# One cross-attention layer on one core: the last batch's output projection is spread over its second pass

## The chip, the core and the metric

The kernel runs on one core of a Trainium2 chip. A core has five engines that run their own instruction streams in order and meet only through semaphores: TensorE (PE) multiplies, with its weight loads shown apart as PEld; VectorE (DVE) and ScalarE (ACT) work on the results; GpSimd (POOL) does copies and subtractions; SyncE (SP) issues most of the DMAs. TensorE writes to PSUM, which has eight banks; the kernel uses all of them. The metric is the device time of one execution in microseconds (us), the median of the runs.

## The reference, cut to what matters

```python
# x, ctx: (8, 256, 1024) float32; Wq, Wout: (1024, 1024); 32 heads of 32
xn = (x - mu) * rsqrt(var + eps) * gamma + beta
Q = split_heads(xn @ Wq.T); K = V = split_heads(ctx)
scores = einsum('bhsd,bhtd->bhst', Q, K) * scale
probs  = softmax(where(mask, scores, -inf))
attn   = einsum('bhst,bhtd->bhsd', probs, V)
return x + attn.reshape(B, S, HIDDEN) @ Wout.T
```

## The kernel before, in words

The eight batches (B = 8) go through a software pipeline, one `iteration` each. The 32 heads are taken four at a time, in G = 8 groups g; a group fills one 128-row slice k = g of the attention result. To keep float32 accuracy with float16 matmuls, `aT`, `woT`, `qT` and the others are kept as a high and a low part, and a product takes three matmuls (`PASSES`).

An iteration has two passes. **First pass**, STEPS = 16 steps n: `scores_s` puts four 128x256 score matmuls into one of the two `score` tiles (score0, score1 in turn, two PSUM banks each); DVE takes the maxima (L826, `max_step`), ACT the exponentials with their sums (L653, `row_sums`). From those come the logarithms of the sums: `lse_half` and `lse_rows` on DVE, `l_transposes` on PE, and `fill_l_rows` on SP, six small DMAs (L203) into `q_stack`, three for each half of the groups. **Second pass**, for each g: `scores_t` twice (L525, four matmuls each, waiting until ACT has emptied the score tile), ACT's `exp_step` twice (L670), then `probs_times_v` (L537) into pv0 or pv1, ACT's copy to `aT` (L676, high part) and DVE's subtraction (L861, low part, semaphore `a_lo`). PE issues `probs_times_v` of g-1 behind the scores of g. ACT issues the copy of g-2 behind the two exponentials of g.

**The output projection** of a batch is 4 tiles of 128x512 (i = 0 to 3), each the sum of 8 slices by 3 passes = 24 matmuls of 512 columns (O_MM = 24, O_ALL = 96). `o_matmuls` (L478) issues them by a unit count u in the order of O_ORDER into the banks mm0 and mm1, i even and odd. `add_residual` (L868) on DVE adds x, `load_res` and `store_out` on SP bring x and take the result. Tiles 2 and 3 wait until the sums of tiles 0 and 1 have been read out of their banks (`o_done`). In the middle of the program the output of batch b-1 is spread over the first pass of batch b, and the query projection of batch b+1 over the second.

In the last iteration (b = 7) there is no next batch. There the output of batch 6 is issued 5 matmuls a step (O_AT_LAST), 80 in all, and the other 16 behind the last step, ahead of the second pass. DVE adds its tiles behind steps 8, 10 and 15 and the fourth behind the loop (O_ADDS_LAST). SP has the store of tile 2 of batch 6 queued ahead of the six L203 DMAs, which the second pass waits for (semaphore l_in). The last batch's own output is 15 matmuls between the `probs_times_v` of groups 6 and 7, and 81 behind that of group 7.

Every wait is written out by hand, and each engine's order is the order of the code.

Of the kernel before, what the change touches and what calls it, by code (L numbers as in the profile page):

```python
# [15 lines left out]
B, S, D = 8, 256, 1024  # L16
H = 32
DH = D // H
P = 128
KT = D // P  # L20
ST = S // P
J = P // DH
G = H // J
LN_EPS = 1e-5
SCALE = float(DH) ** -0.5
W_SCALE = 8.0
# [6 lines left out]
PASSES = ((0, 0), (0, 1), (1, 0))  # L33
FILLS = 4
STEPS = G * ST
# [10 lines left out]
def xattn(nc, x, ctx_in, mask, wq, wout, gamma, beta, out):  # L46
    es = ExitStack()
    with es:
        def sb(name, shape, dt):
            return es.enter_context(nc.sbuf_tensor(name, shape, dt))  # L50

        def sem(name):
            return es.enter_context(nc.semaphore(name))

        wqT = sb("wqT", [P, 2, KT, D], F16)
        woT = sb("woT", [P, 2, KT, D], F16)
# [5 lines left out]
        aT = sb("aT", [P, 2, G, S], F16)  # L62
# [3 lines left out]
        res = sb("res", [P, 2, 512], F32)  # L66
        o_buf = sb("o_buf", [P, 2, 512], F32)
# [27 lines left out]
        score = [es.enter_context(nc.psum_tensor(f"score{i}", [P, J, S], F32)) for i in range(2)]  # L95
        pv = [es.enter_context(nc.psum_tensor(f"pv{i}", [P, 2, S], F32)) for i in range(2)]
        mm = [es.enter_context(nc.psum_tensor(f"mm{i}", [P, 512], F32)) for i in range(2)]
# [22 lines left out]
        t_ready, exp_done, pv_ready = sem("t_ready"), sem("exp_done"), sem("pv_ready")  # L120
        a_hi, a_lo = sem("a_hi"), sem("a_lo")
        o_ready, o_done = sem("o_ready"), sem("o_done")
# [22 lines left out]

        def known(b, n):
            return isinstance(b, int) and b == n

        @block.sync
        def _(sp):  # L150
# [203 lines left out]
        def _(pe):  # L354
# [103 lines left out]
            O_MM = KT * 3  # L458
            O_ORDER = [(0, k) for k in range(7)] + [(1, k) for k in range(4)] + [(0, 7)] + [(1, k) for k in range(4, 8)]
            O_ORDER += [(i, k) for i in (2, 3) for k in range(KT)]  # L460

            def o_matmuls(c, lo, hi, q_before):
                for u in range(lo, hi):
                    (i, k), p = O_ORDER[u // 3], u % 3
                    v = 3 * k + p
                    st, nh = i // 2, i % 2
                    if u == 0:
                        pe.wait_ge(a_lo, c * G + 5)
                    if u in (3 * O_ORDER.index((0, 5)), 3 * O_ORDER.index((0, 6)), 3 * O_ORDER.index((0, 7))):
                        pe.wait_ge(a_lo, c * G + k + 1)  # L470
                    if v == 0 and i >= 2:
                        pe.wait_ge(o_done, c * FILLS + i - 1)
                    elif v == 0 and q_before:
                        pe.wait_ge(q_lo, (c + 1) * FILLS + i + 3)
                    elif v == 0:
                        pe.wait_ge(o_done, (c - 1) * FILLS + i + 3)
                    ap, wp = PASSES[p]
                    last = pe.matmul(mm[i % 2][:], aT[:, ap, k, st * P:(st + 1) * P], woT[:, wp, k, nh * 512:(nh + 1) * 512],  # L478
                                     start=(v == 0), stop=(v == O_MM - 1))
                    if v == O_MM - 1:  # L480
                        last.then_inc(o_ready, 1)

            def scores_s(b, pb, n, first):
                g, st = n // 2, n % 2
                h, gl = divmod(g, HALF)
                if n in (0, STEPS // 2):
                    pe.wait_ge(k_in[h], (b + 1) * (STACK + 1) * DMA)
                if known(b, 0) and n == 0:
                    pe.wait_ge(q0_in, STACK * DMA)
                elif n == (4 if known(b, 0) and h == 0 else h * STEPS // 2):  # L490
                    pe.wait_ge(q_in[h], (b + 1) * STACK * DMA)
                if n >= 2:
                    pe.wait_ge(sum_done, b * STEPS + n - 1)
                elif not first:
                    pe.wait_ge(exp_done, b * STEPS + n - 1)
                else:
                    pe.wait_ge(wq_lo, W_FILLS - 2 + 2 * n)
                for j in range(J):
                    last = pe.matmul(score[n % 2][:, j, :], q_stack[0:S_ROWS, h, j, gl, st * P:(st + 1) * P], k_stack[0:S_ROWS, pb, h, j, gl, :],  # L499
                                     start=True, stop=True)  # L500
                last.then_inc(s_ready, 1)
# [27 lines left out]
            def probs_times_v(b, pb, g):  # L529
                pe.wait_ge(exp_done, b * STEPS + 2 * g + 2)  # L530
                if g < 2:
                    pe.wait_ge(l_done, (b * 2 + g + 1) * L_STEPS)
                else:
                    pe.wait_ge(a_lo, b * G + g - 1)
                for tt in range(ST):
                    for j in range(J):
                        last = pe.matmul(pv[g % 2][DH * j:DH * (j + 1), 0, :], ctx_sb[:, pb, tt, g * P + DH * j:g * P + DH * (j + 1)],  # L537
                                         probs[:, g % 2, tt, j, :], start=(tt == 0), stop=(tt == ST - 1), skip_group_check=True)
                last.then_inc(pv_ready, 1)

            O_ALL, Q_ALL = 4 * O_MM, 4 * Q_MM
            O_AT = [min(7 * n, O_ALL) for n in range(STEPS + 1)]
            Q_AT_STEP = [0] * 14 + [0, 14, 28]
            Q_AT = [60 + 16 * g for g in range(G)] + [182, Q_ALL]
            O_AT_LAST = [5 * n for n in range(STEPS + 1)] + [O_ALL] * (G + 2)
            Q_AT_STEP_FIRST = [0] * 6 + [9 * n for n in range(11)]
            Q_AT_FIRST = [104 + 11 * g for g in range(G)] + [187, Q_ALL]

            def iteration(b, pb, first, last):
                c = None if first else b - 1  # L550
                for n in range(STEPS):
                    scores_s(b, pb, n, first)
                    if not last:
                        if n in Z_STEPS:
                            z_transposes(b + 1, Z_STEPS.index(n), b)
                        if n in K_STEPS:
                            k_transposes(b + 1, 1 - pb, K_STEPS.index(n), b)
                    if first and n in WO_STEPS:
                        wo_transposes(WO_FIRST + WO_STEPS.index(n))
                    if not first:  # L560
                        at = O_AT_LAST if last else O_AT
                        o_matmuls(b - 1, at[n], at[n + 1], True)
                    if not last:
                        at = Q_AT_STEP_FIRST if first else Q_AT_STEP
                        q_matmuls(b + 1, at[n], at[n + 1], c)
                    if n == L_STEP:
                        l_transposes(b, 0, last)
                q_at = Q_AT_FIRST if first else Q_AT
                q_done = Q_AT_STEP_FIRST[STEPS] if first else Q_AT_STEP[STEPS]
                if last:  # L570
                    o_matmuls(b - 1, O_AT_LAST[STEPS], O_AT_LAST[STEPS + 1], True)
                else:
                    q_matmuls(b + 1, q_done, q_at[0], c)
                for g in range(G):
                    scores_t(b, pb, 2 * g)
                    scores_t(b, pb, 2 * g + 1)
                    if not last:
                        q_matmuls(b + 1, q_at[g], q_at[g + 1], c)
                    if g == 0:
                        l_transposes(b, 1, last)  # L580
                    if g >= 1:
                        probs_times_v(b, pb, g - 1)
                if not last:
                    q_matmuls(b + 1, q_at[G], q_at[G + 1], c)
                else:
                    o_matmuls(b, 0, 5 * 3, False)
                probs_times_v(b, pb, G - 1)

            pe.wait_ge(ident_ok, 1)
# [29 lines left out]
            for b in range(1, B - 1, 2):  # L619
                iteration(b, 1, False, False)  # L620
                iteration(b + 1, 0, False, False)
            iteration(B - 1, 1, False, True)
            o_matmuls(B - 1, 5 * 3, O_ALL, False)

        @block.scalar
        def _(act):
# [116 lines left out]
        def _(dve):  # L743
# [119 lines left out]
            def add_residual(c, i):  # L863
                dve.wait_ge(o_ready, c * FILLS + i + 1)
                dve.wait_ge(res_in[i % 2], (c * 2 + i // 2 + 1) * DMA)
                if i >= 2:
                    dve.wait_ge(out_done[i % 2], (c * 2 + 1) * DMA)
                dve.scalar_tensor_tensor(out=o_buf[:, i % 2, :], in0=mm[i % 2][:], scalar=1.0 / W_SCALE, in1=res[:, i % 2, :],  # L868
                                         op0=ALU.mult, op1=ALU.add).then_inc(o_done, 1)

            def iteration(b, first, last, more):
# [45 lines left out]
                    q_split(b + 1, 3)  # L917
                att_split(b, G - 1)

            O_ADDS, O_ADDS_LAST = (6, 8, 11, 14), (8, 10, 15)  # L920
            for r, unit in enumerate(L_UNITS + (1.0,)):
                dve.memset(rows[0:1, r, :], unit).then_inc(consts, 1)
            row_stats(0, 0)
# [7 lines left out]
            for i in range(FILLS):  # L931
# [3 lines left out]
                for m in range(2):  # L935
                    k = 2 * i + m
                    last = dve.tensor_scalar(z0_f32[:, i, m, :], bank[:, m, :], gb[:, 0, k:k + 1], gb[:, 1, k:k + 1], ALU.mult, ALU.add)
# [50 lines left out]
```

## Time and profile before

| | us |
|---|---|
| median of 3 runs | 629.6 (628.39 to 630.53) |
| the profiled execution, its own time | 630.62 |
| its span, first to last instruction | 628.8 |
| last iteration, from the first scores (549.94) to the end | 78.9 |
| of it behind the last attention product's start (606.90) | 21.9 |

Times in the rows below are counted from the start of the span. The trace shows one execution, whose own time is 1.0 us above the median; between span and own time lie 1.8 us. Matmul durations in it are modelled with their drain, so that a group's length is more than its share of the engine; the distance between starts is what the engine takes.

### The profile page before, as it was taken

Reading aid. Unit: us, or ns where it says so; the run is one execution under the profiler, and the core shown is the slowest. Engines: PE = TensorE matmul, PEld = TensorE weight load, DVE = VectorE, ACT = ScalarE, POOL = GpSimd, SP = SyncE. Lnnn points to the kernel's source line nnn. Section 1 sums busy time; section 2 is a strip of 40 time slices with the busy share of each in tenths; the row PEclk is TensorE's granted clock in tenths of the full one; section 3 lists DMA queues with packets and bytes.
Section 4 is the critical chain, followed back from the end, with each engine's and each line's share of the span. In section 5 each row is a group of like instructions: output and inputs, shape, how many; then the busy total and the mean of one; then the engine's idle time right before and its main releaser. Section 6 shows DMA issues by size and latency. Waiting matters only on the chain.

```text
span 628.8 us, 12852 instructions
## 1 busy us (share of the span) xinstructions
PE 589.5 (94%) x4769; PEld 396.2 (63%) x4769; DVE 385.0 (61%) x841; ACT 430.8 (69%) x1321; POOL 112.8 (18%) x131
## 2 busy tenths in 40 slices
PE   4878879999999999999999999999999999998897
PEld 4667657655776567655776567755776567644443
DVE  5575977478654885388654886288645882278211
ACT  3342978778766886678766886678666885699740
POOL 2320440035000530044000520044001520000000
PEclk9889689999999999999999999999999999999899
DMA  9774321443344252343344152333344132321202
GB/s 282 267 223 128 114 73 55 122 126 99 106 117 130 60 163 56 107 117 105 100 125 130 52 170 57 99 119 109 96 124 134 63 89 57 98 51 67 71 1 101
DMA packets 37344, 68.62 MB, mean 109 GB/s; under 512 B 9009, under 2 KB 11041, under 8 KB 37282
## 3 DMA queue, kind: packets, MB, share of 16 engines
q1 hardware_dynamic: 36994, 67.60, 35.9%
q8 instruction: 38, 0.62, 0.4%
q10 hardware_dynamic: 288, 0.20, 0.1%
q14 instruction: 24, 0.20, 0.1%
HBM read 33.56 MB, written 8.39 MB: 67 GB/s over the span
## 4 chain that ended last, share of the span: by engine, by line
PE 71%; DVE 14%; ACT 8%; issue 3%; DMA 2%; ACTq 1%; SPq 1%; DVEq 0%
PE mm L453 24%; PE mm L478 17%; PE pv L537 10%; PE score L525 9%; PE score L499 6%; DVE nmax L826 6%; ACT score L653 6%; PE pv L415 2%; PE pv L428 2%; DMA ctx_sb<-in_ctx 1%; ACT probs L670 1%; DVE o_buf L868 1%; PE pv L382 1%; DVE wqT L748 1%; DVE t_f L777 1%
## 5 line engine op out<-in xcount | busy, mean ns | idle before, releaser
L653 ACT ACTIVATE score<-score,nmax 128x256 f32<-128x256 f32 x512 | 230.1, 465 | 47.7 <-DVE nmax L826 47.6
L453 PE MATMUL mm<-zT,wqT 128*128 128x256 f16 x1536 | 186.6, 276 | 0.0
L826 DVE TENSOR_REDUCE nmax<-score 128x2 f32<-128x512 f32 x256 | 163.8, 684 | 37.0 <-PE score L499 36.9
L478 PE MATMUL mm<-woT,aT 128*128 128x512 f16 x768 | 183.6, 379 | 1.5 <-DVE o_buf L868 1.5
L670 ACT ACTIVATE probs<-score 128x1024 f32<-128x1024 f32 x128 | 123.9, 1022 | 73.4 <-PE score L525 73.1
L453 PEld LDWEIGHTS mm<-zT,wqT 128*128 128x128 f16 x1536 | 151.5, 99 | 23.0 <-issue 2.9
L478 PEld LDWEIGHTS mm<-woT,aT 128*128 128x128 f16 x768 | 74.7, 97 | 73.2 <-DVE o_buf L868 4.4
L653 ACT ACTIVATION_READ_ACCUMULATOR score<-score,nmax 128x1 f32 x512 | 114.7, 224 | 0.0
L861 DVE TENSOR_TENSOR aT<-pv,aT 128x256 f16<-128x256 f32 x64 | 26.9, 423 | 114.7 <-ACT aT L676 113.9
L499 PE MATMUL score<-k_stack,q_stack 97*128 97x256 f16 x512 | 79.6, 279 | 10.5 <-ACT score L653 9.4
L499 PEld LDWEIGHTS score<-k_stack,q_stack 97*128 97x128 f16 x512 | 47.9, 99 | 46.4 <-ACT score L653 22.9
L326 POOL CAST zT<-t_f 128x512 f16<-128x512 f32 x28 | 17.1, 609 | 322.0 <-DVE t_f L769 322.0
L525 PE MATMUL score<-q_stack,k_stack 100*128 100x256 f16 x512 | 68.3, 276 | 2.0 <-ACT probs L670 1.1
L537 PE MATMUL pv<-probs,ctx_sb 128*32 128x256 f32 x1024 | 69.4, 389 | 0.9 <-DVE aT L861 0.6
L525 PEld LDWEIGHTS score<-q_stack,k_stack 100*128 100x128 f16 x512 | 45.7, 98 | 29.2 <-issue 18.1
L537 PEld LDWEIGHTS pv<-probs,ctx_sb 128*32 128x32 f32 x1024 | 27.5, 110 | 25.9 <-ACT probs L670 8.0
L645 ACT ACTIVATE qT<-mm 128x512 f16<-128x512 f32 x32 | 19.5, 608 | 23.0 <-PE mm L453 23.0
L782 DVE SCALAR_TENSOR_TENSOR qT<-mm,qT 128x512 f16<-128x512 f32 x32 | 22.0, 689 | 20.5 <-ACT qT L645 20.0
L328 POOL TENSOR_TENSOR zT<-t_f,zT 128x512 f16<-128x512 f32 x28 | 32.3, 1155 | 2.2
L338 POOL TENSOR_TENSOR kT<-t_f,kT 128x512 f16<-128x512 f32 x28 | 32.3, 1155 | 2.2
L868 DVE SCALAR_TENSOR_TENSOR o_buf<-mm,res 128x512 f32<-128x512 f32 x32 | 21.7, 679 | 17.3 <-PE mm L478 17.3
L676 ACT ACTIVATE aT<-pv 128x256 f16<-128x256 f32 x64 | 24.8, 390 | 9.0 <-PE pv L537 9.0
(62 smaller groups left out, 352.2 us busy)
## 6 DMA issues: line engine op xcount, KB each, us to landing
k_stack<-kT SPq DMA_DIRECT2D x192, 64.0 KB, 2.0
q_stack<-qT SPq DMA_DIRECT2D x180, 64.0 KB, 2.0
x_nat<-in_x SPq DMA_DIRECT2D x8, 1024.0 KB, 5.4
ctx_sb<-in_ctx SPq DMA_DIRECT2D x8, 1024.0 KB, 6.3
res<-in_x SPq DMA_DIRECT2D x32, 256.0 KB, 2.9
out<-o_buf SPq DMA_DIRECT2D x32, 256.0 KB, 2.0
probs<-in_L_xattn_Wq SPq DMA_DIRECT2D x8, 512.0 KB, 7.8
probs<-in_L_xattn_Wout SPq DMA_DIRECT2D x8, 512.0 KB, 4.5
```

Of the source, the lines that this page charges most:

```text
L328: pool.tensor_tensor(zT[:, 1, at], t_f32[:, f % 2], zT[:, 0, at], ALU.subtract).then_inc(split_done, 1)
L338: pool.tensor_tensor(kT[:, 1, at], t_f32[:, f % 2], kT[:, 0, at], ALU.subtract).then_inc(split_done, 1)
L453: last = pe.matmul(mm[i % 2][:, m2 * S:(m2 + 1) * S], wqT[:, wp, k, m * P:(m + 1) * P], zT[:, zp, k, :], start=(v2 == 0), stop=(v2 == KT * ...
L478: last = pe.matmul(mm[i % 2][:], aT[:, ap, k, st * P:(st + 1) * P], woT[:, wp, k, nh * 512:(nh + 1) * 512], start=(v == 0), stop=(v == O_M ...
L499: last = pe.matmul(score[n % 2][:, j, :], q_stack[0:S_ROWS, h, j, gl, st * P:(st + 1) * P], k_stack[0:S_ROWS, pb, h, j, gl, :], start=True ...
L525: last = pe.matmul(score[n % 2][:, j, :], k_stack[0:T_ROWS, pb, h, j, gl, tt * P:(tt + 1) * P], q_stack[0:T_ROWS, h, j, gl, :], start=True ...
L537: last = pe.matmul(pv[g % 2][DH * j:DH * (j + 1), 0, :], ctx_sb[:, pb, tt, g * P + DH * j:g * P + DH * (j + 1)], probs[:, g % 2, tt, j, :] ...
L653: last = act.activation(score[n % 2][:, j, :], score[n % 2][:, j, :], ACT.Exp, bias=nmax[:, st, h, j, gl:gl + 1], accum_out=sums[:, st, h, ...
L670: act.activation(probs[:, g % 2, tt], score[n % 2][:], ACT.Exp).then_inc(exp_done, 1)
L826: dve.tensor_reduce(nmax[:, st, h, at, gl], score[n % 2][:, at, :], AX.X, ALU.max, negate=True).then_inc(max_done, 1)
L861: dve.tensor_tensor(aT[:, 1, g, :], pv[g % 2][:, 0, :], aT[:, 0, g, :], ALU.subtract).then_inc(a_lo, 1)
L868: dve.scalar_tensor_tensor(out=o_buf[:, i % 2, :], in0=mm[i % 2][:], scalar=1.0 / W_SCALE, in1=res[:, i % 2, :], op0=ALU.mult, op1=ALU.add ...
```

## The change

`o_last` and the order `O_GROW` are new; `o_bank` gives tiles 2 and 3 of the last batch the two halves of score0, on PE and on DVE. The output of batch 6 is issued 6 matmuls a step, all 96 in the first pass. DVE adds its tiles behind steps 5, 9 and 13, the fourth behind the loop as before. In the second pass, from g = 2, a piece of six matmuls of the last batch's own output follows `probs_times_v` of g-1: three for tile 0 and three for tile 1, both of slice k = g-2, behind a wait for that slice's `a_lo`. Slices 6 and 7, and the 48 matmuls of tiles 2 and 3, follow the last attention product.

```diff
+        def o_bank(c, i):
+            if known(c, B - 1) and i >= 2:
+                return score[0][:, 2 * i - 4:2 * i - 2].rearrange("p j s -> p (j s)")
+            return mm[i % 2][:]
...
+            O_GROW = [(i, k) for k in range(KT) for i in (0, 1)] + [(i, k) for i in (2, 3) for k in range(KT)]
+            def o_last(lo, hi):
+                c = B - 1
+                for u in range(lo, hi):
+                    (i, k), p = O_GROW[u // 3], u % 3
+                    v = 3 * k + p
+                    st, nh = i // 2, i % 2
+                    if i == 0 and p == 0:
+                        pe.wait_ge(a_lo, c * G + k + 1)
+                    if v == 0 and i < 2:
+                        pe.wait_ge(o_done, (c - 1) * FILLS + i + 3)
+                    elif u == 2 * O_MM:
+                        pe.wait_ge(exp_done, B * STEPS - 1)
+                    ap, wp = PASSES[p]
+                    last = pe.matmul(o_bank(c, i), aT[:, ap, k, st * P:(st + 1) * P], woT[:, wp, k, nh * 512:(nh + 1) * 512],
+                                     start=(v == 0), stop=(v == O_MM - 1))
+                    if v == O_MM - 1:
+                        last.then_inc(o_ready, 1)
...
-            O_AT_LAST = [5 * n for n in range(STEPS + 1)] + [O_ALL] * (G + 2)
+            O_AT_LAST = [6 * n for n in range(STEPS + 1)]
...
-                if last:
-                    o_matmuls(b - 1, O_AT_LAST[STEPS], O_AT_LAST[STEPS + 1], True)
-                else:
+                if not last:
                     q_matmuls(b + 1, q_done, q_at[0], c)
...
+                    if last and g >= 2:
+                        o_last(6 * (g - 2), 6 * (g - 1))
...
-                else:
-                    o_matmuls(b, 0, 5 * 3, False)
                 probs_times_v(b, pb, G - 1)
...
-            o_matmuls(B - 1, 5 * 3, O_ALL, False)
+            o_last(6 * (G - 2), O_ALL)
...
-                dve.scalar_tensor_tensor(out=o_buf[:, i % 2, :], in0=mm[i % 2][:], scalar=1.0 / W_SCALE, in1=res[:, i % 2, :],
+                dve.scalar_tensor_tensor(out=o_buf[:, i % 2, :], in0=o_bank(c, i), scalar=1.0 / W_SCALE, in1=res[:, i % 2, :],
...
-            O_ADDS, O_ADDS_LAST = (6, 8, 11, 14), (8, 10, 15)
+            O_ADDS, O_ADDS_LAST = (6, 8, 11, 14), (5, 9, 13)
```

PE in the second pass of the last batch, before: the scores of one group (into score0 and score1), the attention product of the group ahead of it, and the scores of the next group.

```order
L525 MATMUL score0<-q_stack,k_stack 128x256 [waits exp_done]
L525 MATMUL score0<-q_stack,k_stack 128x256 x3
L525 MATMUL score1<-q_stack,k_stack 128x256 [waits exp_done]
L525 MATMUL score1<-q_stack,k_stack 128x256 x3
L537 MATMUL pv1<-probs,ctx_sb 32x256 [waits a_lo,exp_done]
L537 MATMUL pv1<-probs,ctx_sb 32x256 x7
L525 MATMUL score0<-q_stack,k_stack 128x256 [waits exp_done]
L525 MATMUL score0<-q_stack,k_stack 128x256 x3
```

The same place in the changed kernel, whose line numbers are 28 higher at the scores and the attention product, and where L485 is the matmul of `o_last`.

```order
L553 MATMUL score0<-q_stack,k_stack 128x256 [waits exp_done]
L553 MATMUL score0<-q_stack,k_stack 128x256 x3
L553 MATMUL score1<-q_stack,k_stack 128x256 [waits exp_done]
L553 MATMUL score1<-q_stack,k_stack 128x256 x3
L565 MATMUL pv1<-probs,ctx_sb 32x256 [waits a_lo,exp_done]
L565 MATMUL pv1<-probs,ctx_sb 32x256 x7
L485 MATMUL mm0<-woT,aT 128x512 [waits a_lo]
L485 MATMUL mm0<-woT,aT 128x512 x2
L485 MATMUL mm1<-woT,aT 128x512 x3
L553 MATMUL score0<-q_stack,k_stack 128x256 [waits exp_done]
L553 MATMUL score0<-q_stack,k_stack 128x256 x3
```

Six output matmuls and a wait for `a_lo` now stand ahead of the next group's scores.

DVE at the end of the last batch's first pass, before: the maxima of steps 13, 14 and 15, then the sums of tiles 2 and 3 of batch 6, then `lse_half`.

```order
L826 TENSOR_REDUCE nmax<-score 128x2 [waits s_ready]
L826 TENSOR_REDUCE nmax<-score 128x2
L826 TENSOR_REDUCE nmax<-score 128x2 [waits s_ready]
L826 TENSOR_REDUCE nmax<-score 128x2
L826 TENSOR_REDUCE nmax<-score 128x2 [waits s_ready]
L826 TENSOR_REDUCE nmax<-score 128x2
L868 SCALAR_TENSOR_TENSOR o_buf<-mm,res 128x512 [waits out_done0,res_in0,o_ready]
L868 SCALAR_TENSOR_TENSOR o_buf<-mm,res 128x512 [waits out_done1,res_in1,o_ready]
```

The same place in the changed kernel.

```order
L852 TENSOR_REDUCE nmax<-score 128x2 [waits s_ready]
L852 TENSOR_REDUCE nmax<-score 128x2
L894 SCALAR_TENSOR_TENSOR o_buf<-mm,res 128x512 [waits out_done0,res_in0,o_ready]
L852 TENSOR_REDUCE nmax<-score 128x2 [waits s_ready]
L852 TENSOR_REDUCE nmax<-score 128x2
L852 TENSOR_REDUCE nmax<-score 128x2 [waits s_ready]
L852 TENSOR_REDUCE nmax<-score 128x2
L894 SCALAR_TENSOR_TENSOR o_buf<-mm,res 128x512 [waits out_done1,res_in1,o_ready]
```

The sum of tile 2 has moved ahead of the maxima of steps 14 and 15.

## Rows read from the trace of the kernel before

**Rows 1.** The page, part 1: busy us, share of the span, number of instructions
```profile
PE 589.5 (94%) x4769; PEld 396.2 (63%) x4769; DVE 385.0 (61%) x841; ACT 430.8 (69%) x1321; POOL 112.8 (18%) x131
```
**Rows 2.** Windows of the last batch: stretch, length, busy by engine, clock, DMA
```profile
551.50:582.50 31.00, 27.98 (x151) 13.35 (x150) 23.54 (x44) 30.05 (x132) 0.00 (x0) 1.00 0.22 68
```
**Rows 3.** Timeline, one first-pass step: start, length, engine, line, what [idle before]
```profile
557.18 0.61 PE L499 MATMUL score<-k_stack,q_stack 97*128 97x256 f16 x4
...
557.62 1.25 PE L478 MATMUL mm<-woT,aT 128*128 128x512 f16 x5
...
559.00 0.61 PE L499 MATMUL score<-k_stack,q_stack 97*128 97x256 f16 x4
```
**Rows 4.** Timeline, end of the first pass and start of the second
```profile
575.68 2.47 DVE L826 TENSOR_REDUCE nmax<-score 128x2 f32<-128x512 f32 x4
...
578.20 0.46 ACT L653 ACTIVATE score<-score,nmax 128x256 f32<-128x256 f32 x1
...
580.23 0.68 DVE L868 SCALAR_TENSOR_TENSOR o_buf<-mm,res 128x512 f32<-128x512 f32 x1
...
580.94 0.34 SPq L214 DMA_DIRECT2D out<-o_buf  x1
...
581.33 8.12 SPq L203 DMA_DIRECT2D q_stack<-l_rows  x6
...
582.26 0.23 ACT L663 ACTIVATE ln_e<-ln_s 128x32 f32<-128x32 f32 x1
...
584.41 1.05 PE L525 MATMUL score<-q_stack,k_stack 100*128 100x256 f16 x8 [0.89 <-DMA q_stack<-l_rows]
...
585.06 2.85 ACT L670 ACTIVATE probs<-score 128x1024 f32<-128x1024 f32 x3 [2.57 <-PE score L525]
```
**Rows 5.** Windows around the clock's fall, columns as in rows 2
```profile
583.50:587.00 3.50, 1.90 (x15) 1.19 (x14) 2.33 (x9) 1.94 (x3) 0.00 (x0) 1.00 0.04 9
587.00:590.40 3.40, 3.35 (x23) 1.42 (x24) 0.61 (x2) 1.94 (x2) 0.00 (x0) 0.51 0.04 7
590.80:603.50 12.70, 11.89 (x140) 6.28 (x138) 2.12 (x5) 12.42 (x17) 0.00 (x0) 1.00 0.16 57
```
**Rows 6.** The chain that ended last, behind the clock's fall: start, us, what
```profile
587.05 1.03 PE score L525 x4
588.09 1.86 PE pv L537 x16
589.95 0.83 PE score L525 x4
```
**Rows 7.** Timeline, the second pass at full clock
```profile
593.62 1.07 PE L537 MATMUL pv<-probs,ctx_sb 128*32 128x256 f32 x16 [0.21 <-DVE aT L861]
...
594.62 1.05 PE L525 MATMUL score<-q_stack,k_stack 100*128 100x256 f16 x8
...
595.27 1.94 ACT L670 ACTIVATE probs<-score 128x1024 f32<-128x1024 f32 x2
...
597.09 0.39 ACT L676 ACTIVATE aT<-pv 128x256 f16<-128x256 f32 x1
...
597.52 0.42 DVE L861 TENSOR_TENSOR aT<-pv,aT 128x256 f16<-128x256 f32 x1 [1.93 <-ACT aT L676]
...
598.09 1.07 PE L537 MATMUL pv<-probs,ctx_sb 128*32 128x256 f32 x16 [0.21 <-DVE aT L861]
```
**Rows 8.** Timeline, the tail
```profile
603.56 3.41 PE L478 MATMUL mm<-woT,aT 128*128 128x512 f16 x15
...
606.90 1.07 PE L537 MATMUL pv<-probs,ctx_sb 128*32 128x256 f32 x16
607.90 17.66 PE L478 MATMUL mm<-woT,aT 128*128 128x512 f16 x81
...
608.45 0.42 DVE L861 TENSOR_TENSOR aT<-pv,aT 128x256 f16<-128x256 f32 x1 [3.60 <-ACT aT L676]
...
625.60 0.69 DVE L868 SCALAR_TENSOR_TENSOR o_buf<-mm,res 128x512 f32<-128x512 f32 x1 [4.49 <-PE mm L478]
```

## The prediction, made before the changed kernel was run

> **What bounds the kernel now.** I read the page first: PE is busy for 94% of the span [rows 1], so what matters is where PE is not the limit, and that is the last batch, which has no next batch's projection to fill its waits. The windows show it: in the first pass of the last batch ACT is busy for 30.05 of 31.00 us and PE for 27.98 [rows 2]. Then the timeline of one step: scores start at 557.18, the five output matmuls at 557.62, the next scores at 559.00 [rows 3]. A step is 1.82 us long, set by ACT, and PE needs 0.44 for the scores and 5 x 0.216 = 1.08 for the five (81 of them in 17.66 us less one drain of 0.38 make 0.216 each [rows 8]). So PE rests 0.30 us a step.
>
> At the end of that pass a queue is the limit. DVE adds tile 2 of batch 6 at 580.23, SP stores it at 580.94, and only then issues the six L203 DMAs, from 581.33. The scores of the second pass wait for the first three of them until 584.41, and ACT, done with its logarithm work at 582.49 (582.26 + 0.23), stands idle for 2.57 us before its first exponential at 585.06 [rows 4].
>
> In the second pass a ring of latencies is the limit, not one engine's work. Attention product at 593.62, scores at 594.62, two exponentials from 595.27, the copy at 597.09, the subtraction at 597.52, next but one attention product at 598.09 [rows 7]: 4.47 us for two groups, 2.24 a group. The other group's scores and exponentials lie beside that ring. The tail is PE alone: 15 matmuls, the last attention product, 81 matmuls, up to 625.56 (607.90 + 17.66) [rows 8].
>
> **Term 1, the first pass.** Six matmuls a step make PE's work 0.44 + 1.30 = 1.74 us, still under ACT's 1.82 [rows 3]: cost nothing, with 0.08 us to spare. If the spacing is 0.223, as the 15 have it (603.56 to 606.90 [rows 8]), it is 1.78 and still fits. Upper bound: a twentieth of a us in each of 16 steps, 0.8 us. The 16 matmuls behind the last step are gone from there.
>
> **Term 2, the start of the second pass.** The sum of tile 2 moves ahead of the maxima of step 14. Those of steps 13 and 14 begin at 575.68 and take 2.47 us for four [rows 4], so the sum starts at 575.68 + 1.24 = 576.92. It led to the L203 DMAs 1.10 us after its start and to the scores 4.18 us after it (580.23, 581.33, 584.41 [rows 4]). Moved, it gives scores at 581.10. Then that transfer is no longer last; ACT's own logarithm work is, at 582.49. What is queued behind the moved sum is the maximum of step 14: it starts at 576.92 + 0.68 = 577.60, its first half is done some 0.65 later, at 578.25, and ACT wanted it at 578.20 [rows 4]. I take 0.1 us for that, and 0.7 as the upper bound (all of the sum). The first exponential: 582.6 in place of 585.06, **a gain of 2.46 us**. The stores and loads of x queued on SP behind L203 only come earlier.
>
> **Term 3, the second pass.** Here the order of PE is what counts. The piece of slice g-2 stands behind the scores of g and ahead of the scores of g+1, and waits for `a_lo` of slice g-2. ACT makes that slice's copy only behind both exponentials of g. So the ring is now: scores of g, two exponentials, copy, subtraction, six matmuls, scores of g+1. Nothing of the next group can start beside it, since its scores are behind the wait. From rows 7: scores to exponentials 0.65 (594.62 to 595.27), exponentials to PE's release 2.82 (595.27 to 598.09), six matmuls 1.30. **One group takes 4.77 us in place of 2.24.** The attention product (1.00) lies in the 2.4 us in which PE waits for ACT and DVE, and costs nothing. ACT, busy for 12.42 of 12.70 us in this pass before [rows 5], now waits for PE some 2.5 us a group.
>
> The sum from the first `a_lo` on (593.62 before [rows 7]): five rings 5 x 4.77 = 23.85, the sixth piece 1.30, the last attention product 1.00, then 60 matmuls (slices 6 and 7 and the 48 in score0) 12.96; together 39.11. Slice 7 doesn't delay them: its `a_lo` is ready 2.12 us after the attention product's start (606.90 to 608.45, and 0.57 on to PE as from 597.52 to 598.09 [rows 7, 8]), and that product with slice 6's piece takes 2.30. Before, the same stretch was 593.62 to 625.56 = 31.94. **A loss of 7.17 us.** Below this could go only if PE got past the wait; above it, if a release takes longer (4.6 to 5.0 a ring as bounds, -0.9 to +1.1 in the sum).
>
> **Term 4, the clock.** PE's granted clock was 0.51 (1.2 GHz) from 587.0 to 590.4, after a stretch of 3.50 us in which PE was busy for 1.90; then it came back, PE having been busy without pause [rows 5]. It made three pieces of the path longer: 1.03 against 0.62 for scores, 1.86 against 1.00 for the attention product, 0.83 against 0.62, 1.5 us in all [rows 6]; the short ones are those of rows 3 and 8. In the changed kernel PE has its 16 leftover matmuls no longer, and from some 580.4 to 585.0 runs no more than the scores of two groups and two transposes, waiting for ACT in between. So I expect the same fall, 3 us earlier and at about the same price; it may hit a place where PE waits anyway. I take 0.3 us off. Bounds: -1.5 (it doesn't fall) to +0.5.
>
> **Tail.** The last sum and store are unchanged, and tile 2 comes 24 matmuls (5.2 us) ahead of tile 3 as before. Tiles 2 and 3 wait for nothing.
>
> **Sum:** -2.46 + 7.17 - 0.3 = +4.4 us. On the profiled execution's own 630.62 that is 635.0; on the median of 629.6 it is **634.0**. With every bound at its end, term 1's 0.8 and term 2's other 0.6 among them: from +2.3 to +7.7 us, 631.9 to 637.3.
>
> **Rival A: the clock falls within the rings too.** A ring keeps PE at work for 0.88 + 1.00 + 1.30 = 3.18 of 4.77 us, in two spells with a pause of 1.6 us; before, the second pass had it busy for 11.89 of 12.70 [rows 5] and the clock stayed up. The ring lies between that and the stretch of 583.5 to 587.0, after which it fell, and no row shows which it takes after. A fall doubles the six matmuls and the first scores of a ring, 1.7 us each time. One to four such rings: 1.7 to 7 us, with +4 as the middle: **638**. For it: the pauses come back in every ring. Against it: no single pause is as long as those of 583.5 to 587.0.
>
> The Trainium skill has a rule that speaks for this rival ("TensorE: Matmul & The Clock Gate", section "A second HAM failure mode: psum-queue depth-cycling"): pauses that return between groups of matmuls can make the clock go up and down, and the throughput is lost in the changes. The trace before has such short pauses in each first-pass step at full clock (0.30 of 1.82 us), so it doesn't bear the rule out for pauses of that size, and no row here has a pause of 1.6 us in every group. By that rule the time is the 638 of this rival.
>
> **Rival B, faster: the pieces hide in PE's waits.** That is what they would do if slice g-2 were ready when PE gets to its piece, that is 1.9 us after the scores of g started (0.88 and 1.00) and not 3.47. Then PE's own 3.18 us is the ring, 1.59 less, and five of them give 4.4 - 7.95 = -3.5 us: **626.1**. For it: ACT could copy slice g-2 ahead of g's exponentials, since its product is long done. Against it: the change leaves ACT's order as it is. It breaks even at a ring of 4.77 - 4.4/5 = 3.89 us.
>
> **Rival C: no difference.** The clock doesn't fall at all (-1.2 on my sum), and the rings take 4.5 us, because some release is quicker than in rows 7 (-1.35): +1.8, **631.4**. Each is possible, both together less so.
>
> **Rival D: the first pass no longer holds.** If six matmuls push the steps past ACT's 1.82 us, up to 0.8 us comes on top: 634.8. This lies in the forecast's own range, and has no chance of its own.
>
> **How the numbers follow.** Forecast (631.9 to 637.3) 0.61, rival A 0.23, rival C 0.10, rival B 0.06. A measurement of this kernel can tell about 0.3%, or 1.9 us, from no change. Faster is B, 0.06. Same is C, 0.10. Slower is the rest, 0.84. The range leaves out B and the dearer half of A: 631.0 to 638.5. The predicted time is that of the forecast, 634.0.
>
> **What the profile after would show.** Step by step: (1) first-pass steps still 1.82 us apart with six matmuls in each; a longer step is rival D. (2) L203 issued near 578, the first scores of the second pass near 581.1, ACT's first exponential at 582.6, released by nothing but ACT's own order; if it comes later, the delay of step 14's maximum was more than I took. (3) From then on scores of successive groups 4.8 us apart, PE idle before the pieces for 1.6 us with DVE's L887 subtraction as the releaser, and ACT's exponentials waiting for PE's scores; 3.2 us apart would be rival B. (4) The granted clock at 1.2 GHz once, near 584 to 588; more often and within the rings would be rival A. (5) The last matmul near 630 us of the span. I am wrong on the mechanism, not only on the size, if ACT doesn't wait for PE in the second pass.

## Result and profile after

The changed kernel takes **634.1 us** (median of 6 runs, 633.45 to 635.37), against 629.35 for the kernel before (6 runs, 628.12 to 630.53): a ratio of 1.0079, 95% interval 1.0062 to 1.0096. It is slower by 4.7 us. The forecast was 634.0.

The profiled execution has an own time of 633.76 us and a span of 632.0. In its lines L527 and L553 are the scores of the first and the second pass, L506 is an output matmul of batch 6, L696 an exponential of the second pass, L702 ACT's copy, L887 DVE's subtraction and L894 the sum with x.

The first pass and the start of the second, which [rows 3, 4] show of before. Timeline, columns as there (the first row is the last batch's first scores):

```profile
549.28 0.61 PE L527 MATMUL score<-k_stack,q_stack 97*128 97x256 f16 x4
...
552.88 0.61 PE L527 MATMUL score<-k_stack,q_stack 97*128 97x256 f16 x4
553.33 1.46 PE L506 MATMUL mm<-woT,aT 128*128 128x512 f16 x6
554.70 0.61 PE L527 MATMUL score<-k_stack,q_stack 97*128 97x256 f16 x4
...
576.27 0.67 DVE L894 SCALAR_TENSOR_TENSOR o_buf<-mm,res 128x512 f32<-128x512 f32 x1
...
577.35 9.26 SPq L210 DMA_DIRECT2D q_stack<-l_rows  x6
...
580.44 0.61 PE L553 MATMUL score<-q_stack,k_stack 100*128 100x256 f16 x4 [0.77 <-DMA q_stack<-l_rows]
...
581.79 1.92 ACT L696 ACTIVATE probs<-score 128x1024 f32<-128x1024 f32 x2
```

Steps are 1.82 us apart with six matmuls in each. Counted from the last batch's first scores, the second pass's first scores come 31.16 us in (before: 584.41 - 549.94 = 34.47) and the first exponential 32.51 us in (before: 585.06 - 549.94 = 35.12). ACT no longer stands idle ahead of that exponential.

One ring of the second pass, which [rows 7] show of before (timeline):

```profile
591.12 1.04 PE L553 MATMUL score<-q_stack,k_stack 100*128 100x256 f16 x8
591.76 1.94 ACT L696 ACTIVATE probs<-score 128x1024 f32<-128x1024 f32 x2 [2.46 <-PE score L553]
592.09 1.07 PE L565 MATMUL pv<-probs,ctx_sb 128*32 128x256 f32 x16
593.59 0.39 ACT L702 ACTIVATE aT<-pv 128x256 f16<-128x256 f32 x1
594.01 0.42 DVE L887 TENSOR_TENSOR aT<-pv,aT 128x256 f16<-128x256 f32 x1 [4.25 <-ACT aT L702]
594.49 1.47 PE L485 MATMUL mm<-woT,aT 128*128 128x512 f16 x6 [1.33 <-DVE aT L887]
595.80 1.04 PE L553 MATMUL score<-q_stack,k_stack 100*128 100x256 f16 x8
```

Scores, exponentials, copy, subtraction, six matmuls, scores: 4.68 us for this group (4.67 us between the starts of the pieces). Such a chain, in which each step waits for the one before and the last releases the first of the next group, is called a ring here. PE waits 1.33 us for DVE, ACT 2.46 us for PE. The waits of the second pass and the tail, added up (who waited for whom: us in all, times, longest):

```profile
ACT probs L696 <- PE score L553: 13.7, 7, 2.5
...
PE mm L485 <- DVE aT L887: 8.0, 6, 1.3
```

The tail, which [rows 8] show of before (timeline):

```profile
614.59 1.07 PE L565 MATMUL pv<-probs,ctx_sb 128*32 128x256 f32 x16
615.59 2.76 PE L485 MATMUL mm<-woT,aT 128*128 128x512 f16 x12
...
618.19 10.52 PE L485 MATMUL score<-woT,aT 128*128 128x512 f16 x48
...
628.75 0.69 DVE L894 SCALAR_TENSOR_TENSOR o_buf<-score,res 128x512 f32<-128x512 f32 x1 [4.49 <-PE score L485]
```

PE doesn't stall ahead of slice 7 or of the tiles in score0. The clock, in windows of 1 us (length, PE busy, clock, share and GB/s of DMA):

```profile
582.00:583.00 1.00, 0.56 (x4) 0.91 0.06 16
583.00:584.00 1.00, 1.00 (x6) 0.50 0.03 8
...
586.00:587.00 1.00, 1.00 (x14) 0.89 0.08 16
...
598.00:599.00 1.00, 0.00 (x0) 1.00 0.00 0
```

Before, it fell once too [rows 5]. Here it fell once, from 582.8 to 586.2, and stayed at 1.0 through the six pieces, each with a pause of PE ahead of it (the window from 598.00 lies wholly in one).

**A measure finer than the times.** Executions of one kernel differ by several us: the 21 of the kernel before that front_only is compared with run from 626.48 to 632.24. In the traces most of the difference comes from before the last batch: its first scores stand anywhere from 548.97 to 551.85. So all profiles are compared by the distance from those scores to the start of the last sum (L868 or L894).

| kernel | first scores | first exponential, from there | last sum, from there | clock fell in the last batch |
|---|---|---|---|---|
| before | 549.94 | 35.12 | 75.66 | once |
| changed | 549.28 | 32.51 | 79.47 | once |
| changed, again | 551.48 | 32.51 | 79.59 | once |
| front_only | 551.18 | 32.47 | 72.71 | once |
| growth_only | 550.65 | 35.12 | 80.97 | no |
| wait_only | 549.47 | 32.47 | 79.50 | once |
| early_copy | 550.08 | 32.47 | 69.92 | no |
| early_copy, again | 551.85 | 32.50 | 71.15 | once |
| lag_one | 551.40 | 32.48 | 71.81 | once |
| mm_banks | 549.76 | 32.48 | 79.84 | once |
| clock_kept | 549.13 | 32.47 | 78.30 | no |
| clock_kept, again | 549.30 | 32.50 | 78.32 | no |
| early_fill | 548.97 | 32.50 | 69.95 | no |
| early_fill, again | 550.37 | 32.50 | 69.95 | no |

By it the change costs 79.47 - 75.66 = 3.8 us. The line numbers of the variants below differ by a few from those of the changed kernel.

### The profile page after: what moved, and what is told of

The parts are those of the page before. It is cut to its first block, busy times and chain, and to the rows that moved or that the text cites. A ratio compares the mean times of both kernels' runs of the same rounds, so it can differ in the third digit from the quotient of the medians.

```text
span 632.0 us, 12852 instructions
## 1 busy us (share of the span) xinstructions
PE 587.6 (93%) x4769; PEld 396.8 (63%) x4769; DVE 385.6 (61%) x841; ACT 431.5 (68%) x1321; POOL 113.0 (18%) x131
## 4 chain that ended last, share of the span: by engine, by line
PE 73%; DVE 14%; ACT 7%; issue 3%; DMA 1%; ACTq 1%; SPq 0%; DVEq 0%
PE mm L460 23%; PE mm L506 16%; PE pv L565 9%; PE score L553 9%; PE score L527 7%; DVE nmax L852 6%; ACT score L679 4%; PE mm L485 2%; PE pv L422 2%; ACT probs L696 2%; PE score L485 2%; PE pv L435 2%; DMA ctx_sb<-in_ctx 1%; DVE o_buf L894 1%; DVE wqT L774 1%
## 5 line engine op out<-in xcount | busy, mean ns | idle before, releaser
L696 ACT ACTIVATE probs<-score 128x1024 f32<-128x1024 f32 x128 | 123.9, 1021 | 82.4 <-PE score L553 82.4
L506 PE MATMUL mm<-woT,aT 128*128 128x512 f16 x672 | 162.5, 379 | 1.5 <-DVE o_buf L894 1.5
L679 ACT ACTIVATION_READ_ACCUMULATOR score<-score,nmax 128x1 f32 x512 | 113.4, 221 | 0.0
L506 PEld LDWEIGHTS mm<-woT,aT 128*128 128x128 f16 x672 | 65.5, 97 | 61.4 <-DVE o_buf L894 4.4
L887 DVE TENSOR_TENSOR aT<-pv,aT 128x256 f16<-128x256 f32 x64 | 27.0, 424 | 125.1 <-ACT aT L702 124.4
L527 PE MATMUL score<-k_stack,q_stack 97*128 97x256 f16 x512 | 79.8, 279 | 8.4 <-ACT score L679 8.3
L527 PEld LDWEIGHTS score<-k_stack,q_stack 97*128 97x128 f16 x512 | 47.9, 99 | 43.2 <-ACT score L679 19.8
L553 PE MATMUL score<-q_stack,k_stack 100*128 100x256 f16 x512 | 68.1, 276 | 1.4 <-DMA q_stack<-l_rows 0.8
L553 PEld LDWEIGHTS score<-q_stack,k_stack 100*128 100x128 f16 x512 | 46.3, 98 | 27.3 <-issue 17.3
L702 ACT ACTIVATE aT<-pv 128x256 f16<-128x256 f32 x64 | 24.7, 389 | 8.1 <-PE pv L565 8.1
L795 DVE TENSOR_SCALAR t_f<-pv,gb 128x256 f32<-128x256 f32 x56 | 27.6, 535 | 0.0
```

Of the source, the lines that this page charges most:

```text
L553: last = pe.matmul(score[n % 2][:, j, :], k_stack[0:T_ROWS, pb, h, j, gl, tt * P:(tt + 1) * P], q_stack[0:T_ROWS, h, j, gl, :], start=True ...
L679: last = act.activation(score[n % 2][:, j, :], score[n % 2][:, j, :], ACT.Exp, bias=nmax[:, st, h, j, gl:gl + 1], accum_out=sums[:, st, h, ...
L696: act.activation(probs[:, g % 2, tt], score[n % 2][:], ACT.Exp).then_inc(exp_done, 1)
L795: last = dve.tensor_scalar(t_f32[:, f % 2, m, :], pv[f % 2][:, m, :], gb[:, 0, k:k + 1], gb[:, 1, k:k + 1], ALU.mult, ALU.add)
L887: dve.tensor_tensor(aT[:, 1, g, :], pv[g % 2][:, 0, :], aT[:, 0, g, :], ALU.subtract).then_inc(a_lo, 1)
```

## Experiments

The theory: the new first pass gains 2.5 us; the loss is the wait for `a_lo` that stands in PE's queue ahead of the next group's scores, and not the matmuls behind it. The rivals: the first pass pays for itself; the six matmuls cost because they are ahead of the scores; the clock costs.

### The two halves of the change apart

front_only is the kernel before with

```diff
-            O_AT_LAST = [5 * n for n in range(STEPS + 1)] + [O_ALL] * (G + 2)
+            O_AT_LAST = [6 * n for n in range(STEPS + 1)]
-            O_ADDS, O_ADDS_LAST = (6, 8, 11, 14), (8, 10, 15)
+            O_ADDS, O_ADDS_LAST = (6, 8, 11, 14), (5, 9, 13)
```

and without the 16 matmuls behind the steps.

> The kernel before with the new first pass alone: batch 6's output at 6 matmuls a step, its sums behind steps 5, 9 and 13; the last batch's own output stays 15 + 81 matmuls behind the second pass. Theory (the ring of latencies costs, the first pass gains): 2.5 us faster than before, about 626.9, first exponential of the second pass about 31.9 us after the last batch's first scores, against 35.1 before. Rival (the first pass pays for the sixth matmul and for the delayed maximum of step 14, and the gain is used up by the clock's fall): no faster than 628.7.

Measured: 627.74 us against 629.88, ratio 0.9976 (0.9954 to 0.9998); by the trace 75.66 - 72.71 = 2.95 us less, of which 2.65 are there by the first exponential. Its timeline, at the first exponential and at the last sum:

```profile
583.65 4.07 ACT L668 ACTIVATE probs<-score 128x1024 f32<-128x1024 f32 x4
...
623.89 0.69 DVE L866 SCALAR_TENSOR_TENSOR o_buf<-mm,res 128x512 f32<-128x512 f32 x1 [4.49 <-PE mm L478]
```

The first pass gains what it was taken to gain. The interval of the ratio reaches almost to 1, so the size rests on the trace.

growth_only is the changed kernel with both of those lines, and the 16 matmuls, as they were before.

> The kernel before with the growing tiles and the score banks alone: the first pass stays as it was, 5 matmuls a step, 16 behind it, sums behind steps 8, 10 and 15. Theory: 7.2 us slower than before, about 636.5, with groups 4.7 us apart in the second pass. Rival (the loss of the change comes from what the first pass hands over, its emptier PE and the earlier fall of the clock): under 3 us slower, below 632.4.

Measured: 636.92 us against 629.88, ratio 1.0119 (1.008 to 1.0158): 7.0 us slower. In its trace the pieces of successive groups are 4.67 us apart:

```profile
592.69 1.47 PE L485 MATMUL mm<-woT,aT 128*128 128x512 f16 x6 [1.33 <-DVE aT L889]
...
597.36 1.47 PE L485 MATMUL mm<-woT,aT 128*128 128x512 f16 x6 [1.33 <-DVE aT L889]
```

All of the loss is in this half, and the rival (under 3 us) is out. By the trace it is 80.97 - 75.66 = 5.3 us, but with no fall of the clock in this profile and one in that of before. That fall cost 1.55 us (see "The clock"), so like for like it is 5.31 + 1.55 = 6.9 us.

### The wait without its matmuls

wait_only is the changed kernel with

```diff
-                        o_last(6 * (g - 2), 6 * (g - 1))
+                        pe.wait_ge(a_lo, b * G + g - 1)
...
-            o_last(6 * (G - 2), O_ALL)
+            o_last(0, O_ALL)
```

> The changed kernel with PE's wait for a_lo of slice g-2 left where it stands in the second pass, but with its six matmuls moved behind the last attention product: 96 matmuls there in place of 60. Theory (the wait ahead of the next scores costs, and the matmuls only change places on the same path): the time of the changed kernel, 634.1 within 0.7 us, groups 1.3 us closer (3.4 us apart), and the tail 7.8 us longer. Rival 1 (the six matmuls ahead of the scores are what costs): 4 us or more faster than the changed kernel, below 630. Rival 2 (the clock falls in the rings once PE has longer pauses): over 636, with a granted clock of 0.5 within the second pass.

Measured: 634.47 us, ratio 1.0083 (1.0051 to 1.0116); by the trace 79.50 against 79.47. Its timeline, one ring:

```profile
593.44 1.05 PE L553 MATMUL score<-q_stack,k_stack 100*128 100x256 f16 x8 [1.33 <-DVE aT L887]
594.09 1.94 ACT L696 ACTIVATE probs<-score 128x1024 f32<-128x1024 f32 x2 [1.16 <-PE score L553]
...
596.82 1.05 PE L553 MATMUL score<-q_stack,k_stack 100*128 100x256 f16 x8 [1.33 <-DVE aT L887]
```

The rings are 3.38 us, the scores themselves now wait 1.33 us for DVE, and the 36 matmuls are paid for at the end. By the trace the time is the same to 0.03 us: in the changed kernel the growing pieces hide nothing at all, since in the ring they are on the path just as they are in the tail. The wait alone is the loss: 79.50 against 72.71 of front_only, which has the same first pass and no such wait, is 6.8 us, with one fall of the clock in each.

### The same pieces, with their slice ready

Two ways to have the slice ready. In early_copy ACT copies slice g-2 ahead of the exponentials of g, in the last batch only:

```diff
+                    if last and g >= 2:
+                        att_split(b, g - 2, first)
                     exp_step(b, 2 * g, first)
                     exp_step(b, 2 * g + 1, first)
-                    if g >= 2:
+                    if not last and g >= 2:
                         att_split(b, g - 2, first)
```

> The changed kernel, but in the last batch ACT copies slice g-2 ahead of the two exponentials of group g, not behind them. PE's order is unchanged. Theory: the wait in each ring goes, PE's own work of 3.2 us is the ring; five rings 1.5 us shorter each, and as much again at the first one: 7 to 9.5 us faster than the changed kernel, about 625.5. Rival (the loss is PE's own work and order, whenever the slice is ready): within 1.5 us of the changed kernel, above 632.6.

Measured: 626.52 us against 629.88, ratio 0.995 (0.9929 to 0.9971). Measured again, beside the changed kernel: 626.48 us against 629.4, ratio 0.9943 (0.9924 to 0.9963), 8.75 us under the changed kernel. The timeline of the first, one ring:

```profile
592.24 0.42 DVE L889 TENSOR_TENSOR aT<-pv,aT 128x256 f16<-128x256 f32 x1 [2.85 <-ACT aT L702]
592.63 1.04 PE L553 MATMUL score<-q_stack,k_stack 100*128 100x256 f16 x8
593.27 1.94 ACT L696 ACTIVATE probs<-score 128x1024 f32<-128x1024 f32 x2 [1.06 <-PE score L553]
593.60 1.07 PE L565 MATMUL pv<-probs,ctx_sb 128*32 128x256 f32 x16
594.60 1.47 PE L485 MATMUL mm<-woT,aT 128*128 128x512 f16 x6
595.91 1.04 PE L553 MATMUL score<-q_stack,k_stack 100*128 100x256 f16 x8
```

DVE has the slice ready at 592.66, PE comes to the piece at 594.60, without idle time, and the ring is 3.28 us of PE's own work.

In lag_one the piece is that of slice g-3, and ACT's order is untouched:

```diff
-                    if last and g >= 2:
-                        o_last(6 * (g - 2), 6 * (g - 1))
+                    if last and g >= 3:
+                        o_last(6 * (g - 3), 6 * (g - 2))
```

> The changed kernel with each growing piece one group later: behind the attention product of g-1 stand the six matmuls of slice g-3, from g = 3, whose a_lo is long there; ACT's order stays. 66 matmuls follow the last attention product, not 60. Theory: the same as with the early copy, PE never waits at the piece, the ring is PE's own 3.3 us, about 626.0, 7 to 9 us faster than the changed kernel. Rival (ACT's copying ahead of the exponentials brought the gain of the early copy in some other way than by the wait): within 2 us of the changed kernel, above 632.

Measured: 627.3 us against 630.87, ratio 0.9939 (0.9919 to 0.9959). Its timeline, a piece and the scores of two groups:

```profile
596.43 1.47 PE L485 MATMUL mm<-woT,aT 128*128 128x512 f16 x6
...
597.74 1.04 PE L553 MATMUL score<-q_stack,k_stack 100*128 100x256 f16 x8
...
601.01 1.04 PE L553 MATMUL score<-q_stack,k_stack 100*128 100x256 f16 x8
```

3.27 us a ring again, with ACT in its old order. So it is not the early copy as such, but the wait that it takes away. By the trace, with one fall of the clock in each, lag_one needs 71.81 and early_copy 71.15.

### The banks of tiles 2 and 3

mm_banks is the changed kernel with

```diff
-            if known(c, B - 1) and i >= 2:
-                return score[0][:, 2 * i - 4:2 * i - 2].rearrange("p j s -> p (j s)")
...
-                    elif u == 2 * O_MM:
-                        pe.wait_ge(exp_done, B * STEPS - 1)
+                    elif v == 0:
+                        pe.wait_ge(o_done, c * FILLS + i - 1)
```

> The changed kernel with tiles 2 and 3 of the last batch in mm0 and mm1 again, behind waits for the sums of tiles 0 and 1. Theory (the score banks save one wait at tile 2's start): PE idle for 0.3 to 0.6 us once, ahead of tile 2, nothing ahead of tile 3. Rival (tile 3 waits too): 1 us or more.

Measured: 634.6 us in a single execution, which says nothing of a difference this small; by the trace 79.84 against 79.47. Its timeline, the sums of tiles 2 and 3:

```profile
624.42 0.69 DVE L892 SCALAR_TENSOR_TENSOR o_buf<-mm,res 128x512 f32<-128x512 f32 x1 [4.80 <-PE mm L483]
...
629.60 0.69 DVE L892 SCALAR_TENSOR_TENSOR o_buf<-mm,res 128x512 f32<-128x512 f32 x1 [4.49 <-PE mm L483]
```

DVE waits 4.80 us for tile 2 and 4.49 for tile 3; in the changed kernel it waits 4.49 for each. So tile 2 comes some 0.3 us later and tile 3 waits for nothing more: the score banks save 0.3 to 0.4 us, once.

### The clock

clock_kept is the changed kernel with five more matmuls, of which nothing is used:

```diff
+            def filler(n):
+                for _ in range(n):
+                    pe.matmul(mm[0][:], zT[:, 0, 0, 0:P], wqT[:, 0, 0, 0:512], start=True, stop=True)
...
                     scores_t(b, pb, 2 * g)
+                    if last and g == 0:
+                        pe.wait_ge(o_done, (B - 2) * FILLS + 3)
+                        filler(2)
                     scores_t(b, pb, 2 * g + 1)
+                    if last and g == 0:
+                        filler(3)
```

> The changed kernel with five more matmuls of 512 columns in mm0, whose result is overwritten, in PE's pauses at the start of the second pass: two behind the first scores, three behind the second. Theory (sparse work there lets the clock fall once, at a price of about 1.2 us): the granted clock stays at 1.0 from 575 to the end in the profile, and the time is 1.2 us under the changed kernel's, 632.9. Rival (the fall costs nothing, it lies in PE's wait for the first a_lo): no difference, 634.1, or 0.3 us more.

Measured: 633.59 us against 630.87, ratio 1.0042 (1.0027 to 1.0057); the clock stayed at 1.0 from 575 us to the last matmul. By the trace 78.30 against 79.47, 1.17 us less. By the ratios it was more (1.0079 less 1.0042 of 630 us is 2.3 us), so both were measured again side by side, with the early copy. The timeline of the first, the extra matmuls and ACT's wait for the third group's scores (0.42 us; 1.23 in the changed kernel):

```profile
580.71 0.60 PE L579 MATMUL mm<-wqT,zT 128*128 128x512 f16 x2
...
581.68 0.81 PE L579 MATMUL mm<-wqT,zT 128*128 128x512 f16 x3
...
585.77 1.94 ACT L705 ACTIVATE probs<-score 128x1024 f32<-128x1024 f32 x2 [0.42 <-PE score L553]
```

> The changed kernel again, on one chip and in one go with the three that follow, so that the price of the clock's fall can be read between them. Both theories: 1.007 to 1.009 of the kernel before, as measured.

Measured: 635.23 us against 629.4, ratio 1.0081 (1.0063 to 1.0098).

> The changed kernel with the five extra matmuls. Theory (the fall costs what the rows of the two profiles show between the last batch's first scores and its last sum): 1.1 to 1.4 us under the changed kernel of this go. Rival (the first comparison's 2.3 us by ratios is real, and more than one fall is avoided): 2 us or more under it.

Measured: 633.74 us, ratio 1.0059 (1.0039 to 1.0079): 1.5 us under the changed kernel, by the trace 1.27. The price is the one seen in the rows; the times alone, which spread over 2 to 4 us, couldn't tell it from 2 us. The extra matmuls themselves cost nothing: they lie where PE waits for the scores to be freed and for DVE.

> The early copy again. Theory: 7.5 to 9 us under the changed kernel of this go. Rival: under 7 us.

Measured: 626.48 us, 8.75 us under the changed kernel. Here the profile shows the fall, in the first one it did not: 71.15 against 69.92, 1.23 us. One and the same program is hit in one execution and not in another. Of the eight profiles with the new first pass and without the extra matmuls seven show the fall, of the four with them none.

What a fall costs can be read in a stretch that all these kernels share, from the first exponential to the start of DVE's subtraction for slice 0. Timeline, the subtraction of before (its exponential at 585.06 is in [rows 4]) and after (its exponential at 581.79 is shown above), each behind ACT's longest wait of the stretch; then both ends for growth_only and for clock_kept, neither of which has a fall:

```profile
590.80 1.94 ACT L670 ACTIVATE probs<-score 128x1024 f32<-128x1024 f32 x2 [1.66 <-PE score L525]
593.05 0.42 DVE L861 TENSOR_TENSOR aT<-pv,aT 128x256 f16<-128x256 f32 x1 [5.40 <-ACT aT L676]
...
587.09 1.94 ACT L696 ACTIVATE probs<-score 128x1024 f32<-128x1024 f32 x2 [1.23 <-PE score L553]
589.34 0.42 DVE L887 TENSOR_TENSOR aT<-pv,aT 128x256 f16<-128x256 f32 x1 [4.52 <-ACT aT L702]
...
585.77 3.77 ACT L698 ACTIVATE probs<-score 128x1024 f32<-128x1024 f32 x4 [2.58 <-PE score L553]
592.21 0.42 DVE L889 TENSOR_TENSOR aT<-pv,aT 128x256 f16<-128x256 f32 x1 [3.84 <-ACT aT L704]
...
581.60 3.74 ACT L705 ACTIVATE probs<-score 128x1024 f32<-128x1024 f32 x4
588.01 0.42 DVE L896 TENSOR_TENSOR aT<-pv,aT 128x256 f16<-128x256 f32 x1 [3.34 <-ACT aT L711]
```

With the start of before, it is 7.99 us with the fall (593.05 - 585.06) and 6.44 without (growth_only): the fall costs 1.55. With the start of the changed kernel, 7.55 (589.34 - 581.79) and 6.41 (clock_kept): 1.14. The difference is in ACT's wait for PE's scores, 1.66 against 1.23 us. It is the same 3.4 us at 1.2 GHz; by these rows it costs what ACT has to wait longer for the slowed matmuls.

### Both together

early_fill is the early copy with the five matmuls.

> The changed kernel with both: ACT's copy of slice g-2 ahead of group g's exponentials, and the five extra matmuls. Theory: both gains add, up to 1.2 us under the early copy alone in executions in which its clock falls, about 625.7, no fall of the clock in the last batch, 3.3 us a group. Rival (PE being the limit now, the five matmuls cost their own 1.1 us): 627 or more.

Measured: 624.7 us against 630.87, ratio 0.9904 (0.988 to 0.9928). The rival (627 or more) is out.

> Early copy and the five extra matmuls. Theory: the clock falls in most executions of the early copy too, though not in the one profiled, and its fall costs up to 1.5 us: 0.8 to 1.5 us under the early copy of this go. Rival (it does not fall there, as in its profile): within 0.4 us of it.

Measured: 625.67 us against 629.4, ratio 0.9925 (0.9906 to 0.9945), 0.8 us under the early copy measured beside it. The intervals of the two overlap, and the times don't show this difference. The traces do: 69.95 in both profiles, against 71.15 for the early copy with the fall; and 69.92 for it without the fall says that the five matmuls cost 0.03 us. This is the fastest version of the study, 4 to 6 us under the kernel before and some 9.5 under the changed one (635.23 - 625.67). That its clock never falls is shown only for the two profiled executions.

## Why the prediction was right, step by step

- **The bound and the sign.** The forecast rested on PE's order: a wait in front of the scores that feed ACT. That is what happened; ACT waits for PE in every ring. wait_only shows that this wait alone, with no matmul behind it, gives the whole loss, and early_copy and lag_one show that without it the same pieces are a gain.
- **Term 1, the first pass: nothing.** Right; steps stay 1.82 us apart. Rival D is out.
- **Term 2, the start: -2.46.** It was 35.12 - 32.51 = -2.61. The scores came 3.31 us earlier in the batch, as worked out. ACT began its first exponential 0.14 us after the start of its last logarithm work, which the sum had let it finish first.
- **Term 3, the rings: +7.17.** From the first piece (589.82) to the last matmul's end (618.19 + 10.52 = 628.71) it is 38.89 us, against 31.94 before: +6.95. The ring is 4.67 and not 4.77: from the start of DVE's subtraction to PE it took 0.48 us (594.01 to 594.49), where I had read 0.57 from the attention product in [rows 7]. The matmuls behind the wait are float16 ones here, and the float16 scores behind the wait in wait_only start after 0.48 us too. Five rings are 0.48 less than forecast. The other way, the last piece and the 60 matmuls took 1.40 and 13.12 us for 1.30 and 12.96. The 0.16 of the 60 was a slip of mine: 60 x 0.216 leaves out the drain of the last matmul, which the 31.94 of before contains.
- **Term 4, the clock: -0.3.** It fell once, near where it was expected (582.8 for some 584). From the first exponential to the first slice's release it was 8.03 us (581.79 to 589.82) against 8.56 (585.06 to 593.62): -0.53. Of this 0.09 is the quicker release of term 3, and 0.41 the cheaper fall: 1.14 us after and 1.55 before, as worked out under "The clock". So the 1.5 read off [rows 6] was right for the kernel before, and taking 0.3 off was right in its sign and nearly in its size. The same effect is the rest of front_only's gain: 2.95, of which 2.65 come by the first exponential.
- **The sum.** -2.61 + 6.95 - 0.53 = +3.81 by the trace, where I had +4.41. The medians say +4.74. That the forecast met the median to 0.1 us is better than its terms deserve: they were 0.6 too high against the trace. The match is luck to that extent. Why the times differ by 0.9 us more than the traces do stays open. The median of the kernel before is itself anywhere from 629.35 to 630.87 in the four comparisons. And the clock's fall can give part of it: if the kernel before escapes it in some executions, as growth_only, which has the same first pass, did in its profile, the change costs 3.81 + 1.55 = 5.4 us against those; no run counts how often.
- **Rival A, the clock falls in the rings.** It did not, in either profile of the changed kernel, nor in wait_only, in whose rings PE pauses just as long beside less work. The Trainium skill's rule on pauses that return between groups of matmuls ("TensorE: Matmul & The Clock Gate", section "A second HAM failure mode: psum-queue depth-cycling") doesn't show here: six pauses of 1.33 us, 4.67 us apart, at full clock. The argument that I had against this rival was misread, though. I wrote that no single pause of a ring is as long as those of 583.5 to 587.0; the longest there is the 0.89 us ahead of the scores at 584.41 [rows 4], and every pause ahead of a piece is longer (1.33 us). So the length of one pause doesn't tell in these traces whether the clock falls.
- **Rival B, the pieces hide.** Not in the changed kernel, but its condition was the right one, and early_copy meets it. I had 3.18 us for such a ring and 626.1 for the time; it was 3.28 and 626.5.
- **Rival C, no difference.** Neither half of it came: the clock fell, and a ring took 4.67 us, not 4.5.

## What to carry to other kernels

Work that is moved into an engine's idle time brings its waits along, and in an in-order queue everything behind it waits too. So ask of a filling piece what it waits for, and when that is ready against the moment at which the queue reaches it; here a piece of one group earlier cost nothing, and one whose slice was not yet ready turned an overlap into a ring. And where two placements of the same work are both on the path, its size doesn't matter; only the wait does.

## What was not expected of the hardware

- The last batch's first scores stand up to 2.9 us apart from trace to trace, and all but 0.6 us of that comes from the first 100 us, in which the weights are loaded and batch 0 begins. The last first-pass scores of batch 0 stand from 97.07 to 99.97 in the 14 traces, whereas from there to the last batch's first scores it is 451.6 to 452.2 us in all of them (from 98.09 to 549.94 before, 97.39 to 549.28 after). What varies in those 100 us stays open; the whole spread of the times, 5.8 us among 21 executions, is wider than what these traces hold. Distances inside one trace settled tenths of a us which the times could not.
- Five unused matmuls of 0.2 us each, in pauses at the start of the second pass, went with a granted clock of 2.4 GHz in four profiles of four (seven of the eight without them show the fall) and were worth 1.2 us. The 1.33 us pauses in each later ring never made it fall.
- The same fall of the clock, 3.4 us at 1.2 GHz, cost 1.55 us at one place of the program and 1.14 at another.
